# Attention maxima: for five of a head's sixteen query tiles, one two-input pass over the last two key chunks instead of one maximum over both

## The reference

```
q, k, v = split((x @ w_qkv + b_qkv)); q, k = rope(q), rope(k) beyond the first 679 tokens
attn    = softmax(q @ k.T / sqrt(16));  out = attn @ v;  x = layernorm(x + out @ w_proj + b_proj)
gate, y = fp4_linear(x, w_gate), fp4_linear(x, w_up)
x       = layernorm(x + fp4_linear(silu(gate) * y, w_down))
```

## Time and profile before

| | us |
|---|---|
| median of 3 runs (lowest, highest) | 3718.93 (3711.93, 3724.78) |
| the profiled execution | 3720.92 |
| its span | 3719.1 |

### The profile page before, as it was taken

How to read it: one execution, slowest core, us unless ns; L and a number is a source line. 1 busy time by engine, 2 the same in 40 slices (tenths; PEclk the granted TensorE clock), 3 DMA queues, 4 the chain that set the end, 5 groups by cost and what they waited for, 6 DMA issues and landing times.

```text
span 3719.1 us, 72610 instructions
## 1 busy us (share of the span) xinstructions
PE 3441.3 (93%) x27752; PEld 1547.0 (42%) x27752; DVE 3425.8 (92%) x3879; ACT 2633.9 (71%) x4870; POOL 713.3 (19%) x883
## 2 busy tenths in 40 slices
PE   7769999999999999999999999999999788888887
PEld 4433333333333333333333333333333366666665
DVE  8898999999999999999999999999999298989997
ACT  4442888888888888888888888888888633333333
POOL 6880000000000000000000000000000155555554
PEclk9885999999999999999999999999999899999999
DMA  5451111111111111111111111111111111111110
GB/s 159 141 180 67 40 51 45 40 44 49 43 39 49 46 41 43 50 44 39 47 48 41 41 50 45 40 45 48 43 40 48 43 44 46 45 45 45 45 38 19
DMA packets 121421, 196.69 MB, mean 53 GB/s; under 512 B 28742, under 2 KB 83238, under 8 KB 108838
## 3 DMA queue, kind: packets, MB, share of 16 engines
q1 hardware_dynamic: 111916, 184.26, 14.9%
q10 hardware_dynamic: 9216, 8.39, 0.7%
HBM read 139.55 MB, written 51.38 MB: 51 GB/s over the span
## 4 chain that ended last, share of the span: by engine, by line
PE 69%; issue 10%; POOL 8%; DVE 8%; ACT 2%; DMA 1%; SPq 1%; POOLq 0%; ACTq 0%; DVEq 0%
PE ps L584 35%; PE ps L637 31%; POOL v_all L1168 3%; DVE arena L942 2%; DVE arena L947 1%; POOL arena L1168 1%; POOL arena L1170 1%; ACT arena L801 1%; POOL arena L1162 1%; PE ps L624 1%; POOL arena L1163 1%; ACT arena L810 1%; DVE arena L935 1%; DVE arena L965 1%; PE ps L717 1%
## 5 line engine op out<-in xcount | busy, mean ns | idle before, releaser
L965 DVE TENSOR_REDUCE arena<-ps 128x1 f32<-128x1024 f32 x2048 | 2495.2, 1222 | 114.5 <-PE ps L584 98.3
L810 ACT ACTIVATE arena<-ps 128x512 f32<-128x512 f32 x4096 | 2226.0, 598 | 358.5 <-PE ps L624 273.7
L584 PE MATMUL ps<-kst,qst 48*128 48x512 f32 x4096 | 1519.6, 452 | 27.9 <-DMA qst<-qk_parts 23.6
L624 PE MATMUL ps<-qst,kst 51*128 51x512 f32 x4096 | 1491.1, 447 | 0.0
L637 PE MATMUL ps<-arena 128*32 128x256 f32 x16384 | 1309.5, 392 | 70.5 <-ACT arena L801 66.6
L584 PEld LDWEIGHTS ps<-kst,qst 48*128 48x128 f32 x4096 | 613.9, 188 | 885.4 <-DVE arena L965 718.1
L637 PEld LDWEIGHTS ps<-arena 128*32 128x32 f32 x16384 | 326.3, 108 | 795.4 <-issue 457.0
L624 PEld LDWEIGHTS ps<-qst,kst 51*128 51x128 f32 x4096 | 605.4, 185 | 10.9 <-ACT arena L810 7.4
L1145 POOL TENSOR_TENSOR arena<-arena,ones 128x16 bf16<-128x16 f32 x64 | 14.3, 224 | 2493.6 <-DVE arena L970 2493.6
L727 PE MATMUL ps<-wdT,arena 128*128 128x256 f32 (+1 forms) x768 | 194.3, 405 | 35.3 <-ACT arena L848 35.3
L717 PE MATMUL ps<-wgT,arena 128*128 128x352 f32 x512 | 207.7, 489 | 3.5 <-DVE v_all L1075 2.5
(11 more groups left out here) (101 smaller groups left out, 2295.2 us busy)
## 6 DMA issues: line engine op xcount, KB each, us to landing
qk_parts<-arena SPq DMA_DIRECT2D x32, 1024.0 KB, 7.4
kst<-qk_parts SPq DMA_DIRECT2D x128, 256.0 KB
qst<-qk_parts SPq DMA_DIRECT2D x128, 256.0 KB
kst<-qk_parts SPq DMA_DIRECT2D x128, 128.0 KB
qst<-qk_parts SPq DMA_DIRECT2D x128, 128.0 KB
att<-arena SPq DMA_DIRECT2D x256, 34.0 KB
arena<-in_xT SPq DMA_DIRECT2D x16, 512.0 KB, 8.2
arena<-att SPq DMA_DIRECT2D x128, 64.0 KB
```

What stands on the lines that cost most here:

```text
L584: mm = nc.tensor.matmul(ps[:, i % S_BANKS, :], q[SROW:SROW + STACK, qt * P:(qt + 1) * P], k[SROW:SROW + STACK, kc * CHUNK:(kc + 1) * CHUNK ...
L624: nc.tensor.matmul(ps[:, bank_of_t(g.c, i), :], kst[g.u % 2][first:first + ROWS, kb * P:(kb + 1) * P], qst[g.u % 2][first:first + ROWS, qb ...
L810: nc.scalar.activation(pt[kb % 2][:, qb * CHUNK:(qb + 1) * CHUNK], ps[:, bank_of_t(g.c, i), :], ACT.Exp).then_inc(p_ready, 1)
L965: nc.vector.tensor_reduce(mx[g.u % 2][:, i // 2, i % 2:i % 2 + 1], ps[:, bank:bank + 2, :].rearrange("p b t -> p (b t)"), AX.X, ALU.max).t ...
```

## The change

For heads 8 to 63 and query tiles 2, 5, 8, 11 and 14 of each, the pair of key chunks 2 and 3 is handled in another way. The second S tile of the pair is not q times k of chunk 3 but q times (k of chunk 3 less k of chunk 2). ACT writes its positive part (Relu) to SBUF, behind the Exp of the T tile that stands beside that S tile in PE's order. DVE then makes one `tensor_tensor_reduce`: the scores of chunk 2 from PSUM plus the positive part from SBUF, with the maximum of the sum; an elementwise result of 512 is written too. Since a + max(b - a, 0) is the larger of a and b, the maximum is that of both chunks. DVE waits for ACT's signal `positive` there, and ACT for `s_psum` of the pair (and for DVE's pass two joined pairs back).

The differences of k are made once for each block of eight heads: SP reads the k parts of chunks 2 and 3 (two loads of 512 KB) in head 1 of the block before, POOL makes the difference and its high and low part in four operations before it splits the maxima of head 2, SP stores 2 x 256 KB in head 3, and waits for that in head 6. With S's rows of a head come two more loads (96 KB in all) into `kd` tiles, and PE waits for them at the head's first S tile. `bv_cols` of the first stage moves into a part of `v_all` to make room.

```diff
@@ -70,6 +70,13 @@
 M_AFTER = 51
 HALF_AFTER = (1, 3)
+JOINED = range(2, KT, 3)
+FIRST_JOINED = 8
+LOWEST = -3.4028234663852886e38
 VAR_STEPS = 6
 LN_STEPS = 6
@@ -184,6 +191,20 @@
     return n, slice(0, 8 if n.c >= 8 else 4)
+def joined(g, i):
+    qt = i // CHUNKS
+    if not FIRST_JOINED <= g < G or i % CHUNKS != CHUNKS - 1 or qt not in JOINED:
+        return None
+    return (g - FIRST_JOINED) * len(JOINED) + JOINED.index(qt)
+def joined_pair(n):
+    g, k = divmod(n, len(JOINED))
+    return (g + FIRST_JOINED) * PAIRS + 2 * JOINED[k] + 1
 def each_head(fn):
     for g in range(G):
@@ -223,13 +246,16 @@
         bp_bc = sb("bp_bc", [P, C])
         ones = sb("ones", [P, KT])
         bv_t = sb("bv_t", [P, CT])[:, :]
-        bv_cols = sb("bv_cols", [P, CT, P])
+        bv_cols = v_all[:, 16000:16000 + CT * P].rearrange("p (c t) -> p c t", c=CT)
         arena_words = 22240
         arena = sb("arena", [P, arena_words])
         qst = [sb(f"qst{i}", [SROW + ROWS, N], F32R) for i in range(2)]
         kst = [sb(f"kst{i}", [SROW + ROWS, N], F32R) for i in range(2)]
+        kd_tiles = [sb(f"kd{i}", [SROW + STACK, CHUNK], F32R) for i in range(2)]
+        kd_rows = [t[SROW:SROW + STACK, :] for t in kd_tiles]
         v_view = v_all[:, :].rearrange("p (b h t d) -> p b h t d", b=B, h=H, t=KT)
         def carve(start=0):
@@ -391,6 +427,20 @@
             def load_s(bm, h8):
                 load_rows_of(SROW, h8 % 2, bm, h8, s_in[h8 % 2])
+                if bm:
+                    high, parts = kd_dram[bm, 0, :, h8], kd_dram[bm, 0:PARTS, :, h8]
+                    sp.dma_start(kd_rows[h8 % 2].bitcast(F32)[0:DH], high).then_inc(kd_in[h8 % 2], 16)
+                    sp.dma_start(kd_rows[h8 % 2].bitcast(F32)[DH:STACK], parts).then_inc(kd_in[h8 % 2], 16)
+            def load_differing(bm):
+                for j in range(PARTS):
+                    sp.dma_start(kd_parts[:, j], qk_heads[bm, 1, j].rearrange("s h d (c t) -> (s h d) c t", t=CHUNK)[:, 2:4]
+                                 ).then_inc(kd_src, 16)
+            def store_differences(bm):
+                sp.wait_ge(kd_done, bm)
+                for j, part in enumerate((kd_high, kd_parts[:, 1, 0])):
+                    sp.dma_start(kd_dram[bm, j].rearrange("s h d t -> (s h d) t"), part).then_inc(kd_out, 16)
             def load_t(bm, h8):
                 load_rows_of(MROWS, h8 % 2, bm, h8, t_in[h8 % 2])
@@ -446,6 +496,13 @@
                     if g >= 1:
                         sp.wait_ge(t_psum, bm * (8 * TILES_S) + c * TILES_S)
                     load_t(bm_t, (c + 1) % 8)
+                if bm < G // 8 - 1:
+                    if c == 1:
+                        load_differing(bm + 1)
+                    if c == 3:
+                        store_differences(bm + 1)
+                    if c == 6:
+                        sp.wait_ge(kd_out, 16 * PARTS * (bm + 1))
                 if g < G - 2:
                     sp.wait_ge(s_psum, bm * (8 * PAIRS) + (c + 1) * PAIRS)
                     load_s(bm_s, (c + 2) % 8)
@@ -580,9 +637,13 @@
                 if i % 2 == 0 and not (g.static(0) and pair < 2):
                     pe.wait_ge(s_done, g.times(PAIRS, pair - 1))
                 qt, kc = i // CHUNKS, i % CHUNKS
-                q, k = qst[g.u % 2], kst[g.u % 2]
+                q, k = qst[g.u % 2], kst[g.u % 2][SROW:SROW + STACK, kc * CHUNK:(kc + 1) * CHUNK]
+                if i == 0 and g.c >= FIRST_JOINED:
+                    pe.wait_ge(kd_in[g.c % 2], 32 * ((g.c - FIRST_JOINED) // 2 + 1))
+                if joined(g.c, i) is not None:
+                    k = kd_rows[g.c % 2]
                 mm = nc.tensor.matmul(ps[:, i % S_BANKS, :], q[SROW:SROW + STACK, qt * P:(qt + 1) * P],
-                                      k[SROW:SROW + STACK, kc * CHUNK:(kc + 1) * CHUNK], start=True, stop=True)
+                                      k, start=True, stop=True)
                 if i % 2:
                     mm.then_inc(s_psum, 1)
@@ -800,6 +861,16 @@
                 act.wait_ge(o_store[g.u % 2], g.quad(32 * CHUNKS, 16 * CHUNKS * (g.u // 2 + 1)))
                 nc.scalar.activation(ost[g.u % 2], ps[:, O_BANK, :], ACT.Copy).then_inc(o_out, 1)
+            def positive_part(g, i):
+                n = joined(g, i)
+                if n is None:
+                    return
+                act.wait_ge(s_psum, joined_pair(n) + 1)
+                if n >= 2:
+                    act.wait_ge(s_done, joined_pair(n - 2) + 1)
+                nc.scalar.activation(rises[n % 2], ps[:, i % S_BANKS, :], ACT.Relu).then_inc(positive, 1)
             def head(g):
                 for kb in range(KT):
@@ -809,6 +880,7 @@
                         act.wait_ge(t_psum, g.times(TILES_S, i + 1))
                         nc.scalar.activation(pt[kb % 2][:, qb * CHUNK:(qb + 1) * CHUNK],
                                              ps[:, bank_of_t(g.c, i), :], ACT.Exp).then_inc(p_ready, 1)
+                        positive_part(g.c + 1 + (i + AHEAD) // TILES_S, (i + AHEAD) % TILES_S)
                         if not g.static(0) and kb == 1 and qb == 0:
                             out_of_psum(g.back(1))
                         if i == M_AFTER and not g.static(G - 1):
@@ -962,9 +1034,16 @@
                 for i in range(PAIRS):
                     bank = 2 * i % S_BANKS
                     dve.wait_ge(s_psum, g.times(PAIRS, i + 1))
-                    nc.vector.tensor_reduce(mx[g.u % 2][:, i // 2, i % 2:i % 2 + 1],
-                                            ps[:, bank:bank + 2, :].rearrange("p b t -> p (b t)"), AX.X, ALU.max
-                                            ).then_inc(s_done, 1)
+                    largest = mx[g.u % 2][:, i // 2, i % 2:i % 2 + 1]
+                    n = joined(g.c, 2 * i + 1)
+                    if n is None:
+                        nc.vector.tensor_reduce(largest, ps[:, bank:bank + 2, :].rearrange("p b t -> p (b t)"), AX.X, ALU.max
+                                                ).then_inc(s_done, 1)
+                    else:
+                        dve.wait_ge(positive, n + 1)
+                        nc.vector.tensor_tensor_reduce(out=larger_of, in0=ps[:, bank, :], in1=rises[n % 2], scale=1.0,
+                                                       scalar=LOWEST, op0=ALU.add, op1=ALU.max, accum_out=largest
+                                                       ).then_inc(s_done, 1)
                     if i == PAIRS - 1:
                         dve.wait_ge(s_done, g.times(PAIRS, i + 1))
                         nc.vector.tensor_reduce(nm[g.u % 2], mx[g.u % 2], AX.X, ALU.max, negate=True).then_inc(neg_max, 1)
@@ -1138,8 +1217,22 @@
                 nc.gpsimd.tensor_copy(vs[g.u % 2][:, :, 0:DH], v_all[:, bass.ds(g.times(KT * DH), KT * DH)]
                                       .rearrange("p (t d) -> p t d", t=KT)).then_inc(v_staged, 1)
+            def differences(bm):
+                pool.wait_ge(kd_src, 16 * PARTS * bm)
+                first = 3 * (bm - 1)
+                nc.gpsimd.tensor_tensor(kd_parts[:, :, 1], kd_parts[:, :, 1], kd_parts[:, :, 0], ALU.subtract).then_inc(kd_step, 1)
+                pool.wait_ge(kd_step, first + 1)
+                nc.gpsimd.tensor_tensor(kd_parts[:, 0, 0], kd_parts[:, 0, 1], kd_parts[:, 1, 1], ALU.add).then_inc(kd_step, 1)
+                pool.wait_ge(kd_step, first + 2)
+                nc.gpsimd.tensor_copy(kd_high.bitcast(F32R), kd_parts[:, 0, 0]).then_inc(kd_step, 1)
+                pool.wait_ge(kd_step, first + 3)
+                nc.gpsimd.tensor_tensor(kd_parts[:, 1, 0], kd_parts[:, 0, 0], kd_high, ALU.subtract).then_inc(kd_done, 1)
             def split_maxima(g):
+                if g.c % 8 == 2 and g.c // 8 < G // 8 - 1:
+                    differences(g.c // 8 + 1)
                 p, first = g.u % 2, 3 * g.c
                 pool.wait_ge(neg_max, g.c + 1)
                 nc.gpsimd.tensor_tensor(mp[p][:, 0], nm[p], ones[:, :], ALU.mult).then_inc(m_step, 1)
```

More of the change, by code:

```diff
@@ L206, in layer_kernel @@
         qk_heads = qk_dram.rearrange("b (m k) j s h d t -> (b m) k j s h d t", k=2)
+        kd_dram = nc.dram_tensor("k_differences", (G // 8, PARTS, 2, 8, HALF, CHUNK), F32, kind="Internal").ap()
         att_dram = nc.dram_tensor("att", (G, DH + 1, N), F32, kind="Internal").ap()
@@ L279, in layer_kernel @@
         m_rows = [take(P)[0:MROWS * KT] for _ in range(2)]
+        rises = [take(CHUNK) for _ in range(2)]
+        larger_of = take(CHUNK)
+        take = carve(12 * CHUNK + 8 * CHUNK)
+        kd_parts = take(4 * CHUNK, "p (j c t) -> p j c t", j=PARTS, c=2)
+        kd_high = take(CHUNK)
         take = carve()
@@ L313, in layer_kernel @@
         m_in = [sem(f"m_in{i}") for i in range(2)]
+        kd_in = [sem(f"kd_in{i}") for i in range(2)]
+        kd_src = sem("kd_src")
+        kd_out = sem("kd_out")
         ones_in = sem("ones_in")
@@ L331, in layer_kernel @@
```

(1 more changed line is left out.)

## The result

The changed kernel takes 3880.14 us (median of 4 runs, 3868.82 to 3897.41) against 3717.77 before (4 runs, 3711.93 to 3724.78): a ratio of 1.044, interval 1.0397 to 1.0483, 162 us slower. The prediction was 3849, 130 us slower.

What follows compares the result with a forecast made beforehand. PE was taken to set the time, with ACT setting one stall and DVE following. Per head 4 x 0.52 + 0.18 + 0.06 = 2.32 us, x 56 = 130, on 3720.92 gives 3851; median 2 lower, 3849; range 3805 to 3965.

Steps and rivals of the forecast that it cites:

- PE sets the time and DVE follows: Attention: PE takes one pair every 1.233 us, DVE has 0.3 to 0.4 us in hand, so relieving DVE gains nothing.
- The chain through ACT: Joined pairs: from first matmul start s, two Exps, positive part, DVE pass; PE released s+2.99, due s+2.467, stalling 0.52 us.
- Rival (b): Joined pass on DVE: two-input pass takes 1.22 us or more, stall 0.99, 235 us in all, 3954; chance 14%.
- The joined pair beside T tile 3: One of a head's five joined pairs: its 0.52 us is hidden in the 1.12 stall, which grows by 0.18.
- boundary stall: Once a head, PV on PE waits 1.12 us for ACT's copy of the last head's output, behind an Exp.
- 2.32 us a head, 130 in all: Heads 8 to 63: 4 x 0.52 + 0.18 + 0.06 = 2.32 us a head, x 56 = 130 us.
- The loads and POOL at nothing: Difference loads and POOL's four operations (some 7 us) cost nothing under cover; POOL's would cost 49 us without it.
- the cover that I named: Difference rows asked for 40 us ahead, 1 MB landing in 7.4 us, POOL's work 20 us before the maxima want POOL.
- The clock at its upper level: PE's granted clock in attention, 500 to 2880 us, is 2.4 GHz (granted 1.00).
- The range: Whole kernel: 3805 to 3965 us, leaving out rivals of some 20% with tails; the upper part allows for a slow two-input pass.

Runs made afterwards that it cites:

- e3: Kernel before, with the maxima of 280 pairs covering the first chunk alone (512 elements): 3719.39 us against 3720.12, ratio 0.9999.
- e1: Changed kernel with plain maxima of both chunks and ordinary S tiles; ACT's 280 passes and the loads stay, DVE not waiting for ACT: 3825.93 us, ratio 1.0263.
- e5: Changed kernel without joined passes, loads kept, the next block's 1 MB asked for behind the S and difference rows: 3786.83 us, ratio 1.0172.
- e2: Changed kernel with its loads and POOL's differences, but no ACT pass, plain maxima and ordinary S tiles: 3777.11 us, ratio 1.0167.
- e12: e10 with ACT's copy of the output put ahead of the fifth Exp: 3820.79 us, ratio 1.0283.
- e10: Changed kernel with the 1 MB asked for behind S and difference rows, and POOL's differences behind the maxima split and v staging: 3878.18 us, ratio 1.0434.
- e9: Changed kernel without joined passes, 1 MB asked for behind S and difference rows, POOL's differences behind maxima split and v staging: 3717.99 us against 3717.25.
- e11: e10 with one joined pair a head (query tile 8) instead of five: 3749.87 us, ratio 1.0091.
- e6: Changed kernel with only the next block's 1 MB asked for later, behind the S and difference rows: 3914.15 us, ratio 1.0498.

## Why the prediction was right, and where it was short

- PE sets the time and DVE follows. Right, and shown alone in e3. What the page calls waits for DVE is idle time that stays when DVE gets faster. That the weight loads stand there behind the running PV matmuls is read from the order of the rows, and no run tried it.
- The chain through ACT. Right in place and size: start of the positive part s+1.53 forecast, s+1.51 measured; PE released s+2.99, measured s+3.01. Two errors, of 0.09 and 0.06, nearly cancel in it: from ACT's end to DVE's start I took 0.06, the signal's time between DVE and PE, and it is 0.15; the pass I took at 0.75 and it is 0.69, with the accumulator read inside its tail. The two rows of elementwise passes gave 0.65, a little nearer. Rival (b), a slow pass, did not come: 0.69 us, not 1.22.
- The joined pair beside T tile 3 is hidden in the boundary stall and lengthens it by 0.18. Right: 1.05 idle before PV became 1.23, and e1's heads are 0.18 longer.
- 2.32 us a head, 130 in all. Measured 2.37 a head, 133.
- The loads and POOL at nothing. Wrong, and the cover that I named is the step that failed. I let 1 MB land in 7.4 us, from stores to qk_parts in another stage; in the changed kernel POOL had it 16 to 18 us after its issue, and behind the head's S rows as well it took 22.7 (e5). I let the difference rows be asked for 40 us before PE wants them; it is some 20 (1067.38 to 1088.17 in the changed kernel), and behind the 1 MB they take longer than that. And POOL had not 20 us to spare before the maxima but 5.6 (idle from 1083.8 to 1089.4). In the changed kernel the heads of the loads cost some 10 us, 3.8 of them direct waits of PE (five, of 0.17 to 1.36), 5.3 a fall of the clock behind the longest; in e2, where heads are shorter, the loads cost 57. That the longer heads are what hides the rest was not tried.
- The clock at its upper level. Missed: five falls behind a boundary stall of 1.23, 5.4 us each, 27 us. The prediction named that stall and its growth, but not what may follow it, and no term of the sum stood for it. e12 shows that the falls are gone when this stall is 0.74 us; e1 shows two of them without any of the four others.
- The range. The total, 32 us over the forecast, lies inside it, but by luck: its upper part was made for a slower pass, which did not come, and not for the loads and the clock, which did.

The sum in the profiled execution: 133 + 27 + 10 is 170 over before, attention's first head copy comes 6.6 us earlier there (377.84 instead of 384.4 us), which leaves 163, and the part behind attention is 2.1 shorter, which leaves 161; the spans differ by 160.6. The first copy moves from run to run, from 377.8 to 385.3 us in these profiles, so the 6.6 are not put down to the change.

Why the clock falls behind five boundary stalls and not behind the others stays open: of the 56 in the changed kernel 55 are of 1.23 us, and five of these have a fall behind them; the one of 1.33 has none, while in e10 it has one. The 62 stalls of 1.05 in the kernel before had none, nor those in e9 and e11. Why the 1 MB takes so long behind the S and T rows was not tried either.

## What to carry to other kernels

When two engines are both above 90% busy, look at the distance between starts under disturbance: the engine whose rhythm does not move when the other is late is the bound, and the "wait" beside it is a shadow. The bound is tried by making the other engine's work smaller, as e3 does by leaving 280 second chunks out of the maxima. Taking work off the other engine by way of a third puts that engine's queue into a loop that had slack of 0.4 us; count the loop from signal to signal before counting the work. And a load that "a head's time" hides has to be followed through everything that stands behind it in its own queue and in that of the engine that uses it.

## What the runs showed of the hardware

- Single idle times of PE in a dense stream, of 1.12 us (the shortest, in e6) or more, were in some cases followed by a stretch at 1.2 GHz. Behind the boundary stalls of the changed kernel it was 5 of 55 of 1.23 us, each with some 14 us at the lower level, so that such a stall cost 6.6 us; waits of 1.91 and 2.45 (e2) had none. No stall of 1.05 (before, e3, e9, e11) or 0.74 (e12) had a fall behind it, nor had four stalls of 0.54 a head (e12).
- `tensor_tensor_reduce` runs as two instructions on DVE, 692 ns for 512 elements from PSUM and SBUF, and 83 ns for the read of the accumulator, which overlap: 0.69 us in all (changed kernel, L1044). The Trainium skill, "VectorE: DVE Perf Modes", section "Two Vector instructions with no wait between them", has the two instructions; the trace agrees.
- Relu between Exps loads no function table: neighbours start 0.48 us apart (1528.62, 1529.10), and attention has no table load in the changed kernel's trace. The Trainium skill, "ScalarE: Activation LUTs", section "Table sets: the hidden batching unit", says so, and the trace agrees.
- A signal from ACT was acted on by DVE 0.15 us after ACT's end (1529.70 to 1529.85), one from DVE by PE after 0.06 (1530.54 to 1530.60).
- The two loads of 512 KB landed later when they stood behind more: 16 to 18 us from their issue to the start of POOL's work in the changed kernel, behind T's rows alone, and 22 to 23 in e5, behind S's and the difference rows too.
